# Local scores of layer 0 in two 64-row halves with units in pairs, and the first FFN rows of layer 1 turned ahead of the key-value products

## The reference

```python
# layer 0, attention: windows of 32 queries against 64 keys, 16 heads of 8, plus 64 latents, 8 heads
sc = einsum('bhnid,bhnjd->bhnij', Qb, Kw) / sqrt(8); local = softmax(masked sc) @ Vw
lsc = einsum('bhsd,bhnd->bhsn', GQ, GK) / sqrt(8);   rem = (softmax(masked lsc) @ GV) @ r_out_w
out = (sigmoid(gl) * local + sigmoid(gr) * rem) @ w_out
# layer 0, FFN: the best of 8 experts for each row, gelu(x @ w1 + b1) @ w2 + b2, capacity 256 rows
# layer 1, attention: linear, q = elu(.) + 1, k = elu(.) + 1
kv = einsum('bkhd,bkhm->bhdm', k, v); out = (q @ kv) / max(q . sum(k), 1e-6) @ Wo
# layer 1, FFN: the best 2 of 8 experts for each row
z = (x @ W1 + b1) * (x @ W2 + b2); y = (silu(z @ Wg + bg) * (z @ Wl + bl)) @ W3 + b3
```

## Time and profile before

| what | us |
|---|---|
| median of 3 runs (lowest, highest) | 406.0 (402.62, 406.39) |
| profiled execution, its own time | 403.82 |
| its span in the trace | 401.4 |
| busy in the span: PE, PEld, DVE, ACT, POOL | 352.3, 319.0, 256.6, 177.5, 205.2 |

### The profile page before, as it was taken

How to read it: one execution, slowest core, us unless ns; L and a number is a source line. 1 busy time by engine, 2 the same in 40 slices (tenths; PEclk the granted TensorE clock), 3 DMA queues, 4 the chain that set the end, 5 groups by cost and what they waited for, 6 DMA issues and landing times.

```text
span 401.4 us, 8798 instructions
## 1 busy us (share of the span) xinstructions
PE 352.3 (88%) x2593; PEld 319.0 (79%) x2609; DVE 256.6 (64%) x786; ACT 177.5 (44%) x486; POOL 205.2 (51%) x267
## 2 busy tenths in 40 slices
PE   0899898999999989997897899999999999999910
PEld 0598787988899978876786555999999999999900
DVE  5775998776311669789678897875774444444416
ACT  1715443444556534434454782334334444444304
POOL 8214444898545738692301207444546886642320
PEclk9989999999999999998999989999999999999975
DMA  7781000010362300001010153987888999898137
GB/s 240 268 296 27 0 2 3 21 33 26 106 211 93 123 5 2 0 2 53 19 71 19 53 159 105 308 248 225 264 245 260 287 293 280 288 282 261 69 109 225
DMA packets 33197, 56.01 MB, mean 140 GB/s; under 512 B 4192, under 2 KB 11680, under 8 KB 33152
## 3 DMA queue, kind: packets, MB, share of 16 engines
q1 hardware_dynamic: 28704, 46.14, 36.7%
q0 software_dynamic: 3872, 8.27, 6.3%
q10 hardware_dynamic: 576, 1.05, 0.8%
HBM read 46.59 MB, written 8.85 MB: 138 GB/s over the span
## 4 chain that ended last, share of the span: by engine, by line
PE 62%; DVE 14%; issue 8%; POOL 6%; ACT 4%; DMA 4%; SPq 1%; ACTq 0%; DVEq 0%; POOLq 0%
PE bank L1322 16%; PE bank L1306 8%; PE bank L1035 4%; PE bank L1331 4%; PE bank L997 4%; PE bank L1091 4%; PE bank L1077 3%; DVE rmax L1551 3%; PE bank L1019 2%; PE bank L875 2%; POOL shared L474 2%; POOL shared L468 2%; PE bank L1007 2%; DMA xn<-y_rows 2%; DMA cb<-in_cb 2%
## 5 line engine op out<-in xcount | busy, mean ns | idle before, releaser
L1322 PE MATMUL bank<-kf,shared 128*128 128x128 f32 x624 | 76.0, 275 | 0.0
L1322 PEld LDWEIGHTS bank<-kf,shared 128*128 128x128 f32 x624 | 73.3, 192 | 0.4
L572 POOL DMA_INDIRECT y_rows<-rows,to x39 | 38.5, 988 | 50.6 <-DVE rows L1822 49.6
L1035 PEld LDWEIGHTS bank<-shared 128*128 128x128 f32 x344 | 44.8, 192 | 9.3 <-issue 6.5
L1815 DVE SCALAR_TENSOR_TENSOR we<-bank,bcol,we 128x128 f32<-128x128 f32 x78 | 23.7, 346 | 41.2 <-ACT we L849 39.8
L1035 PE MATMUL bank<-shared 128*128 128x128 f32 x344 | 46.9, 277 | 2.9 <-DVE remn L1595 2.3
L566 POOL DMA_INDIRECT rows<-xn_rows,from x39 | 38.0, 975 | 18.6 <-issue 11.7
L849 ACT ACTIVATE we<-bank,bcol 128x128 f32<-128x128 f32 x78 | 24.4, 364 | 51.6 <-PE bank L1322 51.6
L1551 DVE TENSOR_REDUCE rmax<-bank 128x8 f32<-128x512 f32 (+2 forms) x48 | 30.2, 630 | 26.6 <-PE bank L997 20.0
L1306 PE MATMUL bank<-xtT,shared 128*128 128x128 f32 x312 | 41.4, 276 | 0.5 <-ACT xtT L842 0.4
L1306 PEld LDWEIGHTS bank<-xtT,shared 128*128 128x128 f32 x312 | 38.0, 192 | 1.2 <-ACT xtT L842 0.6
(11 more groups left out here) (258 smaller groups left out, 695.5 us busy)
## 6 DMA issues: line engine op xcount, KB each, us to landing
shared<-in_w1s SPq DMA_DIRECT2D x39, 512.0 KB, 4.7
shared<-in_w1s SPq DMA_DIRECT2D x39, 256.0 KB, 4.1
we<-in_we SPq DMA_DIRECT2D x8, 514.0 KB, 3.4
xn_rows<-xn SPq DMA_DIRECT2D x12, 256.0 KB, 2.4
x<-in_x SPq DMA_DIRECT2D x4, 256.0 KB, 3.6
y_rows<-kf POOLq DMA_DIRECT2D x4, 256.0 KB, 5.8
w1s<-in_w1s SPq DMA_DIRECT2D x2, 512.0 KB, 8.0
xn<-y_rows SPq DMA_DIRECT2D x4, 256.0 KB, 4.2
```

The costliest lines, as they stand in the source:

```text
L572: pool.indirect_dma_start(out=y1_rows, in_=ysb[:, i % 4, :], in_offset=None, out_offset=bass.IndirectOffsetOnAxis(ap=to1[:, i:i + 1].bitca ...
L1035: mm = pe.matmul(bank[4 + g % 2][:, P * i:P * i + P], probT[:, g % 2, P * i:P * i + P], v_, start=True, stop=True)
L1322: mm = pe.matmul(bank[(1, 3)[(k - 1) % 2]][:, P * f:P * f + P], wglb[:, (k - 1) % 4, a, P * f:P * f + P], zT2[:, (k - 1) % 2, a, :], start ...
```

## The change

Local scores. `scores` becomes `local_scores` and `remote_scores`. `local_scores(g)` makes units g and g+1 together, in both score banks: bank h takes what rows 64h to 64h+63 of the array make, that is two of the four groups of heads, for all four windows of the two units. Per pair there are two mask products and eight f32 products of 64 rows by 128 columns, the two halves by turns. `kd` has two copies in place of four, each zero outside every other group of 32 rows; so POOL, ACT and VectorE make two where they made four. It waits for the shift of unit g-1. The values' columns, ACT's copy and the choice of value tile in `weigh` follow the new layout.

Order. The pairs are issued later: in chunk n `local_scores(g + 2)` stands behind queries, keys, latents and `weigh(g - 1)` (before, `scores(g + 2)` stood ahead of the queries); `local_scores(g + 6)` stands behind `project`. VectorE makes `sums(n + 1)`, and in chunk 0 `slot_factors`, ahead of `shift(g + 6)`.

The diff, cut to its core:

```diff
@@ -118,11 +118,11 @@
...
     i = p[:, None] % WIN
-    b["spread"] = p[:, None] == p[None] % WIN
+    b["spread"] = p[:, None] % 64 == p[None] % WIN
     j = np.arange(64)[None]
...
     b["local"] = np.where(np.tile(local, (1, 8)), 0, NEG)
-    b["first"] = np.where(np.tile(np.concatenate([local & (j >= WIN), local], 1), (1, 4)), 0, NEG)
+    b["first"] = np.where(np.tile(np.concatenate([local & (j >= WIN), local, local, local], 1), (1, 2)), 0, NEG)
     cf, cb = np.zeros((P, NCF), np.float32), np.zeros((P, NCB), mybir.dt.np(BF16))
@@ -470,8 +470,8 @@
...
                 pool.wait_ge(s_kT, n + 1)
-                for u in range(4):
-                    pool.tensor_scalar(kd[:, r, u, :], kT[:], c("mine_u", 4)[:, u:u + 1], None, ALU.mult).then_inc(s_kd, 1)
+                for u in range(2):
+                    pool.tensor_scalar(kd[:, r, u, :], kT[:], c("mine_u", 2)[:, u:u + 1], None, ALU.mult).then_inc(s_kd, 1)
 
...
                 act.wait_ge(s_kT, 2)
-                for u in range(4):
-                    act.activation(kd[:, 1, u, :], kT[:], ACT.Copy, scale=c("mine_u", 4)[:, u:u + 1]).then_inc(s_kd1, 1)
+                for u in range(2):
+                    act.activation(kd[:, 1, u, :], kT[:], ACT.Copy, scale=c("mine_u", 2)[:, u:u + 1]).then_inc(s_kd1, 1)
 
@@ -809,16 +810,21 @@
...
 
-            for b_ in range(B):
+            def turned_kv(b_):
                 act.wait_ge(s_kvt, b_ + 1)
...
                 act.copy(kvT[:], bank[5][:, 0:P]).then_inc(s_kvT, 1)
+
+            def projected_kv(b_):
                 act.wait_ge(s_kvw, b_ + 1)
-                act.copy(kvo[:, b_, :], bank[1][:, 0:P]).then_inc(s_kvo, 1)
-
+                act.copy(kvo[:, b_, :], mix_bank[:, 0:P]).then_inc(s_kvo, 1)
+
+            turned_kv(0)
             act.wait_ge(t_x, 1)
             act.copy(xtT[:, 0, :], bank[6][:, 0:P]).then_inc(t_xTs, 1)
+            projected_kv(0)
+            turned_kv(1)
             act.wait_ge(s_route, 2)
@@ -840,6 +846,8 @@
...
                     act.copy(xtT[:, (k + 1) % 2, :], bank[6][:, 0:P]).then_inc(t_xTs, 1)
+                if k == 0:
+                    projected_kv(1)
                 if not single or 1 <= k <= J1:
@@ -975,37 +983,45 @@
...
 
-            def scores(g):
+            def local_scores(g):
                 n, u = divmod(g, U)
-                to, r = bank[g % 2], n % 2
+                r = n % 2
                 if g >= 2:
-                    pe.wait_ge(s_sub, g - 1)
-                if u < UL:
-                    if u == 0:
-                        if n == 0:
-                            pe.wait_ge(s_heads0, 8)
-                        else:
-                            pe.wait_ge(s_qd, 4 * n)
-                        if n == 1:
-                            pe.wait_ge(s_kd1, 4)
-                        elif n:
-                            pe.wait_ge(s_kd, 4 * (n - 1))
-                    mask = "first" if u == 0 and n % NCH == 0 else "local"
-                    pe.matmul(to[:], cbf("spread", P), cbf(mask, 512), start=True, stop=False, skip_group_check=True)
-                    for blk in range(2):
-                        at = WIN * (2 * u + blk)
-                        mm = pe.matmul(to[:].rearrange("p (u b j) -> p u b j", u=4, b=2)[:, :, blk, :],
-                                       qd[:, r, 2 * u + blk].rearrange("p h i -> p (h i)"), kd[:, r, :, at:at + 2 * WIN],
-                                       start=False, stop=(blk == 1), skip_group_check=True)
-                else:
-                    if u == UL:
-                        pe.wait_ge(s_gq, n + 1)
-                        pe.wait_ge(s_gkd, n + 1)
-                    if g == UL:
-                        pe.wait_ge(s_const, 9)
-                    at, nl = n % NCH * CH + P * (u - UL), P // REPS[n % NCH]
-                    mm = pe.matmul(to[:, 0:LH * nl].rearrange("p (h n) -> p h n", h=LH), gqx[:, at:at + P], gkd[:, :, 0:nl], start=True, stop=True)
-                mm.then_inc(s_S, 1)
+                    pe.wait_ge(s_sub, g)
+                if u == 0:
+                    if n == 0:
+                        pe.wait_ge(s_heads0, 6)
+                    else:
+                        pe.wait_ge(s_qd, 4 * n)
+                    if n == 1:
+                        pe.wait_ge(s_kd1, 2)
+                    elif n:
+                        pe.wait_ge(s_kd, 2 * (n - 1))
+                mask = "first" if u == 0 and n % NCH == 0 else "local"
+                for h in range(2):
+                    rows = slice(64 * h, 64 * h + 64)
+                    pe.matmul(bank[h][:], cbf("spread", P)[rows], cbf(mask, 512)[rows], start=True, stop=False, skip_group_check=True)
+                for blk in range(4):
+                    at = WIN * (2 * u + blk)
+                    for h in range(2):
+                        rows = slice(64 * h, 64 * h + 64)
+                        mm = pe.matmul(bank[h][:].rearrange("p (u b j) -> p u b j", u=2, b=4)[:, :, blk, :],
+                                       qd[rows, r, 2 * u + blk].rearrange("p h i -> p (h i)"), kd[rows, r, :, at:at + 2 * WIN],
+                                       start=False, stop=(blk == 3), skip_group_check=True)
+                        if blk == 3:
+                            mm.then_inc(s_S, 1)
+
+            def remote_scores(g):
+                n, u = divmod(g, U)
+                pe.wait_ge(s_sub, g - 1)
+                if u == UL:
+                    pe.wait_ge(s_gq, n + 1)
+                    pe.wait_ge(s_gkd, n + 1)
+                if g == UL:
+                    pe.wait_ge(s_const, 9)
+                at, nl = n % NCH * CH + P * (u - UL), P // REPS[n % NCH]
+                pe.matmul(bank[g % 2][:, 0:LH * nl].rearrange("p (h n) -> p h n", h=LH), gqx[:, at:at + P], gkd[:, :, 0:nl],
+                          start=True, stop=True).then_inc(s_S, 1)
 
@@ -1120,17 +1136,14 @@
...
             turn_x(3)
-            pe.wait_ge(s_xTs, 3)
-            scores(0)
             pe.wait_ge(s_xTs, 4)
-            scores(1)
+            local_scores(0)
             logits0(0)
...
                     turn(g)
-                scores(g + 2)
                 if n == 0:
@@ -1152,8 +1165,8 @@
...
                     weigh(g - 1)
+                local_scores(g + 2)
                 turn(g + 1)
-                scores(g + 3)
                 weigh(g)
@@ -1161,7 +1174,7 @@
...
                 turn(g + 2)
-                scores(g + 4)
+                remote_scores(g + 4)
                 if n == 0:
@@ -1182,15 +1195,13 @@
...
                 turn(g + 4)
-                if more:
-                    scores(g + 6)
                 weigh(g + 3)
...
                     project(n - 1)
+                if more:
+                    local_scores(g + 6)
                 turn(g + 5)
-                if more:
-                    scores(g + 7)
-                else:
+                if not more:
                     pe.wait_ge(s_xTs, 6)
@@ -1275,19 +1286,13 @@
...
             turn_kv(0)
-            project_kv(0)
-            denominators(0)
-            turn_kv(1)
-            keep_warm(3, 2)
-            project_kv(1)
-            keep_warm(3, 2)
-            pe.wait_ge(s_kvo, B)
-            pe.wait_ge(s_bcol, 1)
+            keep_warm(1, 2)
             pe.wait_ge(s_xg[0], 16)
             pe.transpose(bank[6][:, 0:P], xg[:, 0, :], ident).then_inc(t_x, 1)
-            keep_warm(3, 3)
-
+            project_kv(0)
+            turn_kv(1)
             pe.wait_ge(s_w1, 32)
+            pe.wait_ge(s_bcol, 1)
 
@@ -1308,10 +1313,12 @@
...
                     pe.transpose(bank[6][:, 0:P], xg[:, (k + 1) % NXG, :], ident).then_inc(t_x, 1)
+                if k == 0:
+                    project_kv(1)
                 if k % 2 == 0 and k // 2 < NPAIR:
+                    denominators(k // 2)
+                if k % 2 and k // 2 < NPAIR:
                     attention_out(k // 2)
-                if k % 2 and (k + 1) // 2 < NPAIR:
-                    denominators((k + 1) // 2)
                 if not single or 1 <= k <= J1:
@@ -1680,11 +1687,11 @@
...
                 if more:
-                    shift(g + 6)
                     sums(n + 1)
...
                 if more:
+                    shift(g + 6)
                     shift(g + 7)
@@ -1761,8 +1768,7 @@
...
                 dve.sem_inc(s_kvx, 1)
-                if b_ == 0:
-                    query_sum(0)
+            query_sum(0)
 
@@ -1775,8 +1781,6 @@
...
 
-            scaled(0)
-            targets()
             dve.wait_ge(s_b3, 16 * E)
@@ -1795,13 +1799,15 @@
...
                     last.then_inc(t_z, 1)
-                if k in (0, 2, 4):
+                if k == 1:
+                    targets()
+                if k in (1, 3, 5):
                     query_sum(k // 2 + 1)
                 if k % 2 == 0 and k // 2 < NPAIR:
+                    scaled(k // 2)
+                if k % 2 and k // 2 < NPAIR:
                     attention_added(k // 2)
```

(7 more changed lines are left out.)

36 lines of the change are left out of this document (18 added, 18 removed).

## The result

The changed kernel took 412.1 us (median of five runs, 409.2 to 413.2) against 404.4 us in the runs beside it: 1.0187 times as long, 95 % interval 1.014 to 1.0235. It is slower, by about twice what the prediction called the limit of a measurement. The forecast was 402.5 us; the time lies 0.1 us above the range of 393 to 412. The profiled execution took 409.2 us, its span 407.1 (401.4 before). Where the runs of a kernel spread by more than 1.5 %, a ratio here is of its faster runs, while a median is of all of them.

The account below looks back on a forecast made before the run. TensorE was taken to bound an ordinary chunk, VectorE's chain after the change. 403.8 less 0.8 (layer 0) less 0.9 (head of layer 1) gave 402.1 us, 404.3 from the median; 402.5 was taken, range 393 to 412.

Parts of the forecast that it names:

- The pair: Layer 0's local scores: two units' masks and half-array products take 1.3 us, ends 1.1 and 2.4, against 2.16 before.
- L: Length of a pair of units' local scores on TensorE, taken as 1.3 us with streams and loads overlapping.
- rival B: Local scores: weight loads of the two halves do not overlap, pair 2.1 us, kernel 411 us; chance 0.26.
- So the chunk lasts 14.4+0.8+2L = 15.2+2L = 17.8 us: Chunk 3: VectorE's own 14.4 us plus waits of 0.6+L and 0.2+L at its two pairs; 1.4 us won.
- TensorE alone would need ... 17.0: Chunk 3: TensorE's own work in the new order, 18.67-4.3+2.6 = 17.0 us, below VectorE's chain.
- rival A: Layer 0: TensorE's saving lands in full, 16 pairs at 0.86 us, kernel 389 us; chance 0.16.
- Chunks 0 and 1: Start of layer 0: they lose; choice of experts begins at 32.3 instead of 26.46, delay 3.8 us.
- Chunks 2 and 3 return 2.8: Layer 0: these two chunks win back 2.8 us, 1.4 each, of the delay from the first two.
- Chunks 4 to 7: Layer 0 after its experts: gains of 2.15, 0.35 and 0.1 us, then -0.4; together 2.2 us.
- 0.1 us of L is 1.1 us of the kernel: Layer 0: some 11 of 16 pairs stand on the path that ends last, so pair length counts 11 times.
- Part 2: Head of layer 1: rows turned early, FFN tile 0 starts 1.9 us earlier; 0.9 us faster, ends 0 and 2.
- Rival C: New TensorE idle stretches each bring a half-rate clock stretch, costing 4.5 us in all, kernel 407 us; chance 0.12.

Follow-up runs that it names:

- early_pairs: Changed kernel with both score pairs of each chunk issued earlier in TensorE's queue, VectorE's order kept: 402.6 us (396.5 to 404.5).
- cd_early: Changed kernel with both pairs earlier on TensorE, and VectorE's choice of experts and first remote output ahead of the pair's shift: 398.9 us, 0.9869.
- this part alone: Kernel before with only the new head of layer 1, layer 0 as before: 403.3 us, 1.001.
- the fillers: Changed kernel with six filling products in each of three TensorE gaps, in chunk 0 and ahead of chunks 1 and 7: 409.0 us, 1.0158.
- after_again: Changed kernel run again unaltered, beside the run with filling products: 413.5 us, 1.0247.
- attn_only: Changed kernel with the old head of layer 1, so only layer 0 is changed: 413.6 us, 1.0269.
- order_whole: Kernel before with the new order alone, VectorE's included, keeping whole-array score products, four key copies and old layer 1 head: 409.8 us, 1.0155.

## Why the prediction was wrong, point by point

**The pair: right.** L was forecast as 1.3 us and measured as 1.21 plus 0.1. Halves in turn overlap in streams and in loads: 16 passes in 0.98 us (101.19 to 102.17), where rival B wanted 1.7. B is refuted by its mechanism. Its time of 411 is the nearest to the measured one, which shows how little a matching time says of a cause.

**The step that failed: "So the chunk lasts 14.4+0.8+2L = 15.2+2L = 17.8 us".** It lasted 19.31. VectorE's waits at the two pairs were 2.25 and 1.98 us, not 1.9 and 1.5: 0.8 us more. Two waits for the remote scores, 0.88 and 0.25, together 1.1 us, were not in the sum at all. VectorE's own part was 13.95 (19.31 less the four waits), not 14.4. That makes up the 1.5 us. At the second pair the sum let `project` follow the mix at once, but the weighing of 99.53 stands ahead of it in TensorE's queue, so it starts at 100.42, 0.7 us behind the mix and not 0.2. The walk also took TensorE's queue between the pairs as never waiting. But the prediction itself had VectorE idle 1.9 us ahead of the shift of the pair, and behind that shift, in an in-order queue, stands the remote output that frees the bank of the next weighing. So TensorE stands 1.45 us, and comes later to the next pair. The prediction read this step for the experts in chunk 0 and not for the remote output in chunks 1 to 7. It is the smaller part: with it removed chunk 3 is 0.5 us shorter, of the 1.5, and the kernel's time did not change by anything that could be told (411.5 us); with the choice of experts moved too some 4.5 us came back. What removed the loss and more was to bring the pair earlier. Either order leaves two engines waiting for each other in turn; `early_pairs` lets VectorE's other work cover the pair.

**"TensorE alone would need ... 17.0": right**, 17.03 in `cd_early`. The saving of rival A was there to be had, but not in the order of this change.

**Chunks 0 and 1: about right in size.** The choice of experts was forecast at 32.3 and begins at 32.12; 3.8 us later at chunk 1 was forecast, 4.3 measured at its gates (49.03 against 53.30). A part of it may be the clock of 0.83. "Chunks 2 and 3 return 2.8" failed, by the step above: they took 1.5 more.

**Chunks 4 to 7: half right.** From chunk 3's gates to chunk 6's 1.6 us were won (the table's 0.8, 0.1 and 0.7), where 2.2 were forecast: 2.15, 0.35 and 0.1, less 0.4 ahead of the experts. Then 1.4 were lost up to chunk 7's gates where 0.4 was forecast, with a pair of 2.25 us in the slow stretch.

**"0.1 us of L is 1.1 us of the kernel": wrong in this order, half right in the other.** A pair longer by 0.55 us cost nothing that could be told here (412.0 against 412.1 us) and 6 us with early pairs, where 11 pairs by 0.55 would be 6.0.

**Part 2: right in its steps, 0.9 us too high in its sum.** Tile 0 came 1.75 us earlier (1.9 forecast), TensorE then waits 1.47 us for the division (1.7 forecast), and the gate product is not early at all (0.3 forecast). The waits of the later tiles that should have gone were not worth anything in the end: 1.001 (0.9987 to 1.0033) for this part alone.

**Rival C, the clock: right in mechanism, lucky in size, given too small a chance.** It was priced at 4.5 us, and the fillers returned 4.5. But C counted on three places: ahead of the first pair, the end of chunk 0 and tile 1. Of these only the end of chunk 0 was slower than before in the profiled execution: over 20 to 30 us both kernels have 0.86, and tile 1 has 1.00. The others that were slower are chunk 7 and the stretch ahead of tile 0 (0.72 against 0.86), and the fillers stood in chunks 0, 1 and 7. The clock is not a rival to the waits but their second cost. Of the 9.8 us between `after_again` and the kernel before, 4.5 go with three gaps filled (in part a loss of the kernel before too), and 5.4 stay. How much of those 5.4 is clock in other stretches was not measured. The clock would also explain why `attn_only` (413.6 us) is slower than `order_whole` (409.8 us), whose pair is 0.9 us longer: their profiled runs have a mean granted clock of 0.945 and 0.968. That they differ by this alone is argued from the fillers, and was not measured.

## What to carry to other kernels

When a change makes one engine wait longer in an in-order queue, list everything that stands behind the waiting instruction and who waits for it, in every stage and not only in the first; then move the work whose inputs are ready ahead of the wait, and bring the awaited product forward. A product made shorter saved nothing that could be told here while the engine that takes its result was idle for it. That its shorter time comes back as idle time that lowers the clock is a suspicion left from `attn_only` and `order_whole`, not a measurement. To see whether halves, copies or a shorter product are worth having, measure them once in an order in which their engine is full.

## What the runs showed of the hardware

Two 64-row halves of the array overlap their f32 products, weight loads included, when products for the two halves alternate: 16 passes over 128 columns in 0.98 us (101.19 to 102.17), where one behind another they would need 1.76. The 16 loads fit into it too, at 0.061 us each, where the loads of the logits took 0.107. The Trainium skill, TensorEngine Tiling, section Key Properties, says that different tiles load and multiply in parallel, and this trace agrees. With eight passes of one half and then eight of the other they took 1.53 us (101.43 to 102.96), so little is left of the overlap. Going from the whole array to halves costs about 0.1 us: the four passes of 100.42 at 0.11 us would end at 100.86, and the mask starts at 100.96. The way back was not measured apart; it lies within the 0.98 us.

Adding products that compute nothing made the kernel faster. In the changed kernel TensorE stood 2.05 us ahead of the turn at 190.06, and the window behind it reads (TensorE alone)

```profile
192.00:196.00 4.00, 4.00 (x24) 0.50 0.00 0
```

which is the lower of the two levels, 1.2 GHz. With the fillers that gap was 0.77 us long, and the clock stayed at 1.00. The gap of 1.82 us in chunk 0 (ahead of 36.48, with 1.14 us more ahead of 37.89) was followed by a shorter drop, 0.65 over 38 to 42; cut to 0.55 us it was followed by none. The gap of 1.78 us ahead of chunk 1 was followed by none, so that not every gap costs. The Trainium skill, TensorE: Matmul & The Clock Gate, section What's actually happening, says that a gate passes half or all of the clock's pulses by how busy TensorE has been, and these rows agree in that. Within one kernel the times follow the clock: of the six runs of `early_pairs`, two took 396.5 and 398.8 us at a mean clock of 0.967, and three took 404.1 to 404.5 us at 0.951.
